# Attention scores from one fp32 product of queries and keys, in place of three products of split parts: a gated attention and mixture-of-experts block

## What is computed

```
q = _ln(q, qln_w, qln_b)
k = _ln(k, kln_w, kln_b)
scores = jnp.einsum('bsghd,btgd->bghst', q, k) * scale
p = jax.nn.softmax(scores, axis=-1)
return jnp.einsum('bghst,btgd->bsghd', p, v)
```

## Time and profile before

| | |
|---|---|
| median of 3 runs | 798.06 us (796.53 to 799.0) |
| profiled execution, its own time | 796.67 us |
| its span, first to last instruction | 794.9 us |
| mean granted TensorE clock | 0.989 of full speed |
| PE busy | 717.0 us, 90% of the span, 4913 instructions |
| PEld busy | 584.5 us, 74% |
| DVE busy | 604.7 us, 76%, 1286 instructions |
| ACT busy | 466.3 us, 59%, 1179 instructions |
| POOL busy | 448.1 us, 56%, 585 instructions |

### The profile page before, as it was taken

How to read it: one execution, slowest core, us unless ns; L and a number is a source line. 1 busy time by engine, 2 the same in 40 slices (tenths; PEclk the granted TensorE clock), 3 DMA queues, 4 the chain that set the end, 5 groups by cost and what they waited for, 6 DMA issues and landing times.

```text
span 794.9 us, 15421 instructions
## 1 busy us (share of the span) xinstructions
PE 717.0 (90%) x4913; PEld 584.5 (74%) x4913; DVE 604.7 (76%) x1286; ACT 466.3 (59%) x1179; POOL 448.1 (56%) x585
## 2 busy tenths in 40 slices
PE   3748899899999989999998999998978799999996
PEld 3646787778888778888886878877856666777775
DVE  6867888788898869788887888888888783454444
ACT  5646867677686766768677676866655232222221
POOL 2425777566767756677776667776866315222220
PEclk9979999999999999999999999999999999999999
DMA  6310100100001010001001010000002015666661
GB/s 186 113 54 1 33 23 1 54 28 28 1 27 29 1 54 28 27 1 28 28 2 52 3 34 2 27 1 2 1 1 61 21 48 148 192 194 190 189 186 54
DMA packets 44479, 42.76 MB, mean 54 GB/s; under 512 B 3717, under 2 KB 43386, under 8 KB 44410
## 3 DMA queue, kind: packets, MB, share of 16 engines
q1 hardware_dynamic: 41706, 36.61, 15.1%
q0 software_dynamic: 1536, 5.28, 2.5%
q10 hardware_dynamic: 1168, 0.01, 0.1%
HBM read 39.52 MB, written 2.37 MB: 53 GB/s over the span
## 4 chain that ended last, share of the span: by engine, by line
PE 63%; DVE 18%; ACT 7%; issue 6%; POOL 4%; ACTq 1%; DMA 0%; POOLq 0%; DVEq 0%
PE out_ps L1760 8%; PE s_ps L1531 7%; PE proj_ps L1487 6%; PE pT_ps L1540 6%; PE proj_ps L1472 6%; PE aux_ps L1550 5%; PE aux_ps L1564 5%; DVE q_tok L1103 5%; PE aux_ps L1501 4%; PE proj_ps L1463 4%; POOL rstd L528 3%; PE work_ps L1752 3%; DVE ss L1083 2%; PE work_ps L1774 2%; PE aux_ps L1408 2%
## 5 line engine op out<-in xcount | busy, mean ns | idle before, releaser
L543 POOL TENSOR_SCALAR p_sb<-p_sb,psum_row 128x256 f32<-128x256 f32 x256 | 125.5, 507 | 67.6 <-DVE psum_row L1122 66.3
L798 ACT ACTIVATE p_sb<-s_ps,negmax 128x256 f32<-128x256 f32 x256 | 118.5, 473 | 64.0 <-DVE negmax L1117 62.8
L1550 PE MATMUL aux_ps<-pT_sb,v_sb 128*128 128x512 f32 x256 | 120.7, 593 | 4.0 <-DVE pT_sb L1128 4.0
L1531 PE MATMUL s_ps<-kT,qT 128*128 128x256 f32 x768 | 112.3, 289 | 8.2 <-DVE qT L1113 4.6
L1128 DVE COPY pT_sb<-pT_ps 128x512 f32<-128x512 f32 x128 | 87.6, 685 | 41.2 <-PE pT_ps L1540 40.5
L550 POOL TENSOR_TENSOR y_bf<-y_bf,mg_bf 128x512 bf16<-128x512 bf16 x64 | 85.9, 1342 | 58.4 <-DVE mg_bf L1140 58.3
L1531 PEld LDWEIGHTS s_ps<-kT,qT 128*128 128x128 f32 x768 | 97.6, 190 | 18.3 <-issue 18.3
L1117 DVE TENSOR_REDUCE negmax<-s_ps 128x2 f32<-128x512 f32 x128 | 86.4, 683 | 5.9 <-PE s_ps L1531 5.6
L528 POOL TENSOR_TENSOR rstd<-var,minus_half 128x8 f32<-128x8 f32 (+1 forms) x64 | 85.7, 1339 | 5.3
L553 POOL TENSOR_TENSOR catq<-y_bf,mg_bf 128x512 fp32r<-128x512 bf16 x64 | 79.6, 1243 | 5.0
L1564 PE MATMUL aux_ps<-wpT,catq 128*128 128x256 f32 x512 | 69.1, 288 | 5.9 <-DVE wkvT L1031 4.8
(11 more groups left out here) (188 smaller groups left out, 1394.9 us busy)
## 6 DMA issues: line engine op xcount, KB each, us to landing
w_up_a<-in_L_ffn_gate_up_proj SPq DMA_DIRECT2D x16, 384.0 KB, 3.5
w_up_b<-in_L_ffn_gate_up_proj SPq DMA_DIRECT2D x16, 384.0 KB, 3.6
wp_raw<-in_L_xattn_wproj SPq DMA_DIRECT2D x16, 256.0 KB, 2.9
w_down_a<-in_L_ffn_down_proj SPq DMA_DIRECT2D x16, 192.0 KB, 3.7
w_down_b<-in_L_ffn_down_proj SPq DMA_DIRECT2D x16, 192.0 KB, 3.6
w_raw<-in_L_xattn_w_kv_x SPq DMA_DIRECT2D x8, 256.0 KB, 4.6
w_raw<-in_L_xattn_wq SPq DMA_DIRECT2D x7, 256.0 KB, 2.7
w_raw<-in_L_xattn_wqx SPq DMA_DIRECT2D x7, 256.0 KB, 3.0
```

Of the source, the lines that this page charges most:

```text
L543: ins = nc.gpsimd.tensor_scalar(p_sb[:, r, st, :], p_sb[:, r, st, :], rsum[:, r, st:st + 1], 1.0, ALU.mult, ALU.mult)
L798: ins = nc.scalar.activation(p_sb[:, r, st, :], s_ps[:, r % 2, st, :], ACT.Exp, bias=negmax[:, r, st:st + 1], accum_out=psum_row[:, r, st: ...
L1531: ins = nc.tensor.matmul(s_ps[:, k % 2, st, :], qT[:, a, ty, h, st * P:(st + 1) * P], kT[:, b, ty, s.gi, :], start=(i == 0), stop=(i == 2))
L1550: ins = nc.tensor.matmul(aux_ps[:, f.bank, :], v_sb[:, (2 * s.n + tt) % VRING, ty, s.gi, :], pT_sb[:, ty, :, tt, :], start=(tt == 0), stop ...
```

## The change

The full queries and keys are kept as fp32 and multiplied once. `evac_Tq` and `evac_Tk` write directly into `qT` and `kT`; the rounding copies on ACT (`q_hi`, `k_hi`) and the subtractions on DVE (`qk_lo`) are gone, 96 of each (64 for queries, 32 for keys). The waits that stood in front of `q_hi` and `k_hi`, for the scores that last read `qT` or `kT`, now stand in front of the evacuations. PE no longer waits for `qk_lo`, but for the evacuation itself (`wait_drained`). `qk_f` stays for another use at the start. `qT` and `kT` are half as large.

```diff
-        qT = sb("qT", [P, 2, NTYPE, HPG, SEQ], F32R)
-        kT = sb("kT", [P, 2, NTYPE, 2, SEQ], F32R)
+        qT = sb("qT", [P, NTYPE, HPG, SEQ])
+        kT = sb("kT", [P, NTYPE, 2, SEQ])
...
-                wait(act, qk_lo_ready["TX" if ty == 0 else "TQ"], s.a + ty)
+                wait(act, s_ready, s.m - (0 if ty else 2))
                 w = QW + 2 * ty
-                nc.scalar.activation(qk_f[:, 0, :], aux_ps[:, f.bank, :],
+                nc.scalar.activation(qT[:, ty, :, :].rearrange("p a b -> p (a b)"), aux_ps[:, f.bank, :],
                                      ACT.Identity, scale=vec[:, w:w + 1], bias=vec[:, w + 1:w + 2]
                                      ).then_inc(aux_free[f.bank], 1)
...
-            def q_hi(s, ty):
-
-                x = "TX" if ty else "TQ"
-                f = Fill(x, s.a)
-                act.wait_ge(aux_free[f.bank], f.drained)
-                wait(act, s_ready, s.m - (0 if ty else 2))
-                full, (hi, lo) = qk_parts(x)
-                nc.scalar.activation(hi, full, ACT.Copy).then_inc(qk_hi_ready[x], 1)
...
-            def qk_lo(n, x):
-
-                dve.wait_ge(qk_hi_ready[x], n + 1)
-                full, (hi, lo) = qk_parts(x)
-                nc.vector.tensor_tensor(lo, full, hi.bitcast(F32), ALU.subtract).then_inc(qk_lo_ready[x], 1)
...
             def scores(s, k):
 
                 ty, h = k // 2, k % 2
-                pe.wait_ge(qk_lo_ready["TKx" if ty else "TKs"], s.n + 1)
-                pe.wait_ge(qk_lo_ready["TX" if ty else "TQ"], s.a + 1)
+                wait_drained(("TKx" if ty else "TKs", s.n), ("TX" if ty else "TQ", s.a))
...
                 for st in range(TPB):
-                    for i, (a, b) in enumerate(((0, 0), (0, 1), (1, 0))):
-                        ins = nc.tensor.matmul(s_ps[:, k % 2, st, :], qT[:, a, ty, h, st * P:(st + 1) * P],
-                                               kT[:, b, ty, s.gi, :], start=(i == 0), stop=(i == 2))
+                    ins = nc.tensor.matmul(s_ps[:, k % 2, st, :], qT[:, ty, h, st * P:(st + 1) * P],
+                                           kT[:, ty, s.gi, :], start=True, stop=True)
                 ins.then_inc(s_ready, 1)
```

More of the change, by code:

```diff
@@ L222, in flamingo_kernel @@
         qk_normed = sem("qk_normed")
-        qk_hi_ready = {x: sem(f"qk_hi_ready_{x}") for x in ("TQ", "TX", "TKs", "TKx")}
-        qk_lo_ready = {x: sem(f"qk_lo_ready_{x}") for x in ("TQ", "TX", "TKs", "TKx")}
         s_ready = sem("s_ready")
@@ L373, in flamingo_kernel @@
         block = ctx.enter_context(nc.Block())
[L376 to L381, removed]
         VECTORS = [("L0_xattn_ln_w", 0), ("L0_xattn_ln_b", 2), ("L0_xattn_q_in_scale", 4), ("L0_xattn_k_in_scale", 6),
@@ L769, in evac_Tk @@
                 act.wait_ge(aux_filled, f.filled)
-                wait(act, qk_lo_ready["TKx" if ty == 0 else "TKs"], n + ty)
+                wait(act, s_ready, 8 * n - (0 if ty else 2))
                 w = KW + 2 * ty
-                nc.scalar.activation(qk_f[:, 1, :], aux_ps[:, f.bank, :],
+                nc.scalar.activation(kT[:, ty, :, :].rearrange("p a b -> p (a b)"), aux_ps[:, f.bank, :],
                                      ACT.Identity, scale=vec[:, w:w + 1], bias=vec[:, w + 1:w + 2]
                                      ).then_inc(aux_free[f.bank], 1)
-            def q_hi(s, ty):
-                x = "TX" if ty else "TQ"
-                f = Fill(x, s.a)
-                act.wait_ge(aux_free[f.bank], f.drained)
-                wait(act, s_ready, s.m - (0 if ty else 2))
-                full, (hi, lo) = qk_parts(x)
-                nc.scalar.activation(hi, full, ACT.Copy).then_inc(qk_hi_ready[x], 1)
[L785 to L790, removed]
-                full, (hi, lo) = qk_parts(x)
-                nc.scalar.activation(hi, full, ACT.Copy).then_inc(qk_hi_ready[x], 1)
             def exps(s, r):
@@ L841, in _ @@
                     evac_Tk(s1.n, 1)
-                    k_hi(s1.n, 1)
                 if kv:
@@ L856, in _ @@
                 if s1:
-                    q_hi(s1, 1)
                     exps(s1, 0)
@@ L869, in _ @@
                     evac_Tk(s0.n, 0)
-                    k_hi(s0.n, 0)
                 if s1:
@@ L876, in _ @@
                     evac_Tq(s0, 0)
-                    q_hi(s0, 0)
                 if i == NSUB:
@@ L1235, in _ @@
                     maxes(s1, 1)
-                    qk_lo(s1.a, "TX")
                     recip(s1, 0)
@@ L1269, in _ @@
                     x1_norm(i - NSUB + 1)
-                if s0 and s0.gi == 0:
-                    qk_lo(s0.n, "TKs")
                 if s1:
@@ L1274, in _ @@
                     magic(s1, 0)
[L1275 to L1279, removed]
                     evac_pT(s1, 3)
```

## The result

The changed kernel takes 807.22 us (median of 4 runs, 806.77 to 807.83), the kernel before 798.53 us in the same session (4 runs, 796.53 to 799.29): ratio 1.0113, 95% interval 1.0092 to 1.0134. It is slower, as forecast, and 0.7 us above the forecast time. The profiled execution took 807.83 us, with a span of 806.0 us.

The account below looks back on a forecast made before the run. PE was taken to bound the kernel, DVE and ACT mattering only where PE waits. 19.0 - 1.9 - 1.8 - 5.5 = +9.8 us on the profiled 796.67 gave 806.5 us, range 801 to 812.

Parts of the forecast that it names:

- The product: Scores on PE: 16 fp32 instructions of 0.215 us replace 24 fp32r products of 0.119 per sub, +19.0 us in 32 subs.
- The wait for the queries: PE's wait at L1501 for scaled queries: longer scores 3 fill idle time in twelve turns of the loop, -1.9 us.
- Scores 2 in turns with keys: PE's wait before scores 2 for the context queries' subtraction goes, six times 0.31, -1.8 us.
- The 8.2 us before scores: PE's idle time before scores over the whole run: -5.5 us expected back, with 0 and 8.2 as the ends.
- The place at 553.57: One of two PE waits for a subtraction behind DVE's statistics in the last turns: 1.0 us expected back.
- the last sub's first scores: Start of the last two subs' scores, where PE waited for a subtraction: all 1.9 us expected to go.
- the drain: Pipeline draining after the last place where PE waits before scores: 0.5 us more expected back.
- the start: PE's 1.5 us wait for an exponential at the start: 0.3 of longer scores hidden, 0.3 of a copy lost, 0.6.
- The place at 587.87: PE's wait before scores 2 behind two subtractions and DVE statistics: scores 2 start 2.2 earlier, 1.5 us counted here.
- Nothing comes back: Rival: PE's waits keep their length because other work, above all the maxima, ends at the same time; 815.7 us, chance 0.12.
- The relief pays: Rival: with DVE and ACT work removed, the L1501 wait falls away in all loop turns; 792.9 us, chance 0.06.
- The new waits in front of the evacuations: Evacuations wait for the scores that last read qT and kT, at least some microseconds back; costed at nothing.

Follow-up runs that it names:

- the product alone: Kernel before with scores as one fp32 product, but every rounding copy, subtraction and wait kept, their results unread: 811.68 us, ratio 1.016.
- the relief alone: Changed kernel with three fp32r products per score block again, all on rounded high parts, copies and subtractions still gone: 795.23 us, ratio 0.995.
- the fourth experiment: Changed kernel with the sums and statistics on DVE moved ahead of the rounding step that feeds POOL, in three turns: 808.55 us in one run.

## Why the prediction was right, point by point

**The product, +19.0.** The distance of 0.215 is borne out: 1.73 for eight, 0.86 for four. In a turn without special waits it came to 0.594 us where I had 0.59, 19.0 us in 32 subs (my own 32 x 0.59 is 18.9). Only its "two instructions, each as long as two passes" is too round: 0.215 is 1.8 times the 0.119 of an fp32r product.

**The wait for the queries, -1.9.** Right in size and in cause: twelve turns, 0.40 left of 0.56, 2.2 us together, nothing in the others. That scores 3 hide it, and not the relief, is shown by the product alone, where the wait falls to 17.9, and by the relief alone, where it stays at 19.9.

**Scores 2 in turns with keys, -1.8.** Nearly right in size, 6 x 0.26 = 1.6, but I gave the subtraction that goes as what ends the wait. Either part of the change is enough: with the relief alone these six turns are 0.27 shorter than before, and with the product alone the subtraction is still there and the six waits are not, since the longer scores 0 and 1 hide them.

**The 8.2 us before scores, -5.5.** This is the term that I mis-sized; it gave 4.5. The place at 553.57 gave 0.8 for 1.0, the last sub's first scores 1.3 and those of the one before it 1.2 for 1.9 together, the drain 0.3 for 0.5, the start 0.7 for 0.6. The place at 587.87 gave 0.2, no more than the longer scores 0 and 1 that are hidden in it, where my sum had 1.5: from scores 0 to scores 2 it is 587.87 - 581.55 = 6.32 us before and 599.90 - 593.58 = 6.32 after. My step was that scores 2 start 2.2 earlier once the subtractions are out of the way. The whole turn did move up, but the two sums ahead of the maximum came to lie beside POOL's roundings and took 2.30 in place of 1.17, which is most of what is missing. That they take 0.87 away from POOL is shown by the fourth experiment.

**What had no term.** The values of the second sub wait 0.88 for a copy out of PSUM where they waited 1.32, and L1363 in three turns 0.80 for L785 on ACT where it waited 0.94. Together 0.8 us came back here that my sum doesn't have.

So 19.0 - 2.2 - 1.6 - 4.5 - 0.8 = 9.9 us, against 9.94 in the trace and a forecast of 9.8. The product came as forecast, and 9.1 us came back of the 9.2 that I had. That this agrees so well is in part luck: the term before the scores was 1.0 too large, and waits that I had not looked at made up for most of it. Between the medians it is 8.7 us, since the profiled run before lies below its median and the one after above.

**The rivals.** Nothing comes back asked for 815.7, 8.5 us above what was measured, and even with no operation removed 5.8 us came back. The relief pays needs most of the wait for the queries to go; it went from 20.2 to 19.9. The new waits in front of the evacuations, which I costed at nothing, do not show as a wait of PE for an evacuation.

**DVE and ACT.** I expected 65 us less on DVE and 61 on ACT; it is 60.5 and 51.7. Busy time is a union, and the removed operations overlapped their neighbours: in the kernel before a copy runs from 581.01 for 0.63 and the evacuation behind it starts at 581.55. No term of the sum rests on it.

## What to carry to other kernels

Work taken from engines that are not the bound is worth only the waits that it ends: here 96 operations on each of two engines, 112 us of their busy time, came to 3 or 4 us between the medians. Work put on the engine that is the bound is hidden only where it already waits, and work taken from it comes back only until the next chain that stands directly behind it (13 of 61 us). So list the waits of the bounding engine one by one, ask of each what is late next, and look at what the freed engine's work will then lie beside.

## What the runs showed of the hardware that was not expected

Operations with two inputs on DVE and on POOL hold each other up. POOL's roundings, by line, after the change and then before:

```profile
L541 POOL TENSOR_TENSOR y_bf<-y_bf,mg_bf 128x512 bf16<-128x512 bf16 x64 | 74.4, 1163 | 66.4 <-DVE mg_bf L1103 66.4
...
L544 POOL TENSOR_TENSOR catq<-y_bf,mg_bf 128x512 fp32r<-128x512 bf16 x64 | 74.4, 1162 | 5.0
```

```profile
L550 POOL TENSOR_TENSOR y_bf<-y_bf,mg_bf 128x512 bf16<-128x512 bf16 x64 | 85.9, 1342 | 58.4 <-DVE mg_bf L1140 58.3
...
L553 POOL TENSOR_TENSOR catq<-y_bf,mg_bf 128x512 fp32r<-128x512 bf16 x64 | 79.6, 1243 | 5.0
```

With DVE's subtractions gone they take 1163 and 1162 ns on average, with them 1342 and 1243; with the relief alone, where they are gone too, it is 1161 and 1162, and with the product alone, where they stay, 1341 and 1239. On DVE the sums take 0.87 alone and 2.30 beside POOL's roundings, and the subtraction of the keys 1.35 beside a rounding where a subtraction takes 0.68. A copy out of PSUM on DVE beside the same rounding of the changed kernel is not stretched: it starts at 593.93 and takes 0.69. The Trainium skill, "SBUF — State Buffer", section "SBUF: two separate sides", says that a DVE operation with two inputs in SBUF and a GpSimd operation take a pair of ports from each other for a whole instruction. The trace agrees in direction and nearly in size. This rounding stands beside the subtraction of the keys, before the change:

```profile
580.94 1.53 POOL L550 TENSOR_TENSOR y_bf<-y_bf,mg_bf 128x512 bf16<-128x512 bf16 x1 [1.35 <-DVE mg_bf L1140]
```

By that rule the subtraction that starts at 581.67 would be held until 582.47 and take 0.80 + 0.68 = 1.48, an estimate; it takes 1.35.

The granted clock fell to the lower level behind waits of PE of 1.9 and 3.0 us in the relief alone, but not behind those of 1.6 and 2.7 us in the changed kernel, nor behind 2.4 and 2.15 us in the kernel before. What decides it was not tried. Each such stretch cost 1.2 to 1.5 us where it was looked at (two in the relief alone, one each in the product alone and in the fourth experiment), so a difference of that size between two single runs can be the clock's.
